# All x tiles asked for first, six at a time, with the adjacency of block 0 and the masks of unit 0 moved behind them

## The reference

```
h   = x @ W                      per head: 2048 x 64
s1  = h @ a1,  s2 = h @ a2       one score per node and head
e   = leaky_relu(s1[i] + s2[j], slope 0.2)
att = softmax over j of (e where adj[i, j] > 0, else -9e15)
out = layernorm(x + concat over heads of (att @ h))
```

## Time and profile before

| | |
|---|---|
| median of 3 runs | 3051.29 us |
| profiled execution | 3049.79 us |
| its span | 3048.1 us |
| busy: PE, VectorE, ScalarE, GpSimd | 2650.5, 2729.3, 2417.2, 841.0 us |
| L473, the products of h | 462.1 us |
| L574, ScalarE's compares | 2179.6 us |
| L807 + L814, the masks on VectorE | 616.5 + 583.9 us |

### The profile page before, as it was taken

How to read it: one execution, slowest core, us unless ns; L and a number is a source line. 1 busy time by engine, 2 the same in 40 slices (tenths; PEclk the granted TensorE clock), 3 DMA queues, 4 the chain that set the end, 5 groups by cost and what they waited for, 6 DMA issues and landing times.

```text
span 3048.1 us, 94883 instructions
## 1 busy us (share of the span) xinstructions
PE 2650.5 (87%) x36162; PEld 2275.6 (75%) x36162; DVE 2729.3 (90%) x4505; ACT 2417.2 (79%) x4038; POOL 841.0 (28%) x1011
## 2 busy tenths in 40 slices
PE   4898889989898898988989889898888988889885
PEld 2498875888668885788848888488874988758885
DVE  4899988999889998899988999889998999889996
ACT  2399973999649995599937998389973999739994
POOL 3522116121252213322143221512215121162211
PEclk9999999999999999999999999999999999999998
DMA  6346633575435654267542665337644476345763
GB/s 167 87 104 163 160 103 97 127 168 141 116 83 131 163 137 136 56 155 165 131 111 68 161 163 127 97 84 166 160 112 112 100 160 159 103 105 120 165 144 89
DMA packets 281095, 388.25 MB, mean 127 GB/s; under 512 B 161856, under 2 KB 161856, under 8 KB 280672
## 3 DMA queue, kind: packets, MB, share of 16 engines
q1 hardware_dynamic: 253536, 315.24, 39.3%
q0 software_dynamic: 27136, 67.12, 12.8%
HBM read 313.52 MB, written 34.14 MB: 114 GB/s over the span
## 4 chain that ended last, share of the span: by engine, by line
DVE 40%; issue 25%; PE 23%; ACT 6%; DVEq 2%; POOL 0%; DMA 0%; ACTq 0%; POOLq 0%
DVE m_pos L807 8%; PE ps L473 8%; PE ps L499 7%; DVE both L644 7%; PE ps L529 6%; ACT m_pos L574 6%; DVE m_pos L793 5%; DVE both L634 3%; DVE total L650 3%; DVE m_neg L814 2%; DVE xmax L625 2%; DVE y L674 2%; DVE prod L776 1%; DVE prod_d L779 1%; PE ps L410 1%
## 5 line engine op out<-in xcount | busy, mean ns | idle before, releaser
L574 ACT ACTIVATE m_pos<-ps,s_steep 128x512 fp8e4<-128x512 f32 x3584 | 2179.6, 1081 | 419.9 <-PE ps L424 309.6
L499 PE MATMUL ps<-b_both,m_pos 128*128 128x130 f16 x16384 | 1030.2, 223 | 242.0 <-DVE both L634 220.4
L499 PEld LDWEIGHTS ps<-b_both,m_pos 128*128 128x128 fp8e5 x16384 | 978.6, 99 | 275.0 <-issue 273.8
L529 PE MATMUL ps<-d_both,m_neg 128*128 128x130 f16 x16384 | 989.8, 222 | 46.5 <-DVE both L644 46.1
L529 PEld LDWEIGHTS ps<-d_both,m_neg 128*128 128x128 fp8e5 x16384 | 966.5, 99 | 74.2 <-issue 64.1
L807 DVE TENSOR_TENSOR m_pos<-m_pos,maskT 128x1024 uint32<-128x1024 uint32 x512 | 616.5, 1242 | 78.0 <-ACT m_pos L574 44.0
L814 DVE TENSOR_TENSOR m_neg<-m_pos,maskT 128x2048 uint32<-128x2048 uint32 x256 | 583.9, 2281 | 0.4
L473 PE MATMUL ps<-W_sb,xT 128*128 128x512 f32 x1024 | 462.1, 613 | 39.6 <-DVE prod_d L779 39.6
L540 ACT ACTIVATE adj_cut<-adj_in 128x1024 fp8e4<-128x1024 int32 x264 | 363.7, 1429 | 130.1 <-DMA adj_in<-in_adj 130.1
L970 POOL TENSOR_TENSOR den_scaled<-den_inv,bound 128x4 f32<-128x4 f32 x256 | 62.2, 243 | 1456.7 <-DVE den_inv L652 1396.1
L473 PEld LDWEIGHTS ps<-W_sb,xT 128*128 128x128 f32 x1024 | 200.4, 197 | 295.7 <-issue 240.5
(11 more groups left out here) (89 smaller groups left out, 1396.1 us busy)
## 6 DMA issues: line engine op xcount, KB each, us to landing
adj_in<-in_adj SPq DMA_DIRECT2D x266, 512.0 KB, 5.0
s_bc<-s_rows SPq DMA_DIRECT2D x258, 256.0 KB, 3.8
x_in<-in_x SPq DMA_DIRECT2D x144, 256.0 KB, 5.2
x_sum<-in_x POOLq DMA_DIRECT2D x128, 256.0 KB, 5.9
y<-in_x POOLq DMA_DIRECT2D x32, 1024.0 KB, 9.8
out<-y SPq DMA_DIRECT2D x32, 1024.0 KB, 7.3
maskT<-adj_cut SPq DMA_TRANSPOSE x264, 4.2
W_sb<-in_L_gnn_W SPq DMA_DIRECT2D x4, 256.0 KB, 7.2
```

The source lines that it names most:

```text
L499: mm = pe.matmul(acc, mask, b_both[:, j, h, :, :], start=(j == 0), stop=(j == JC - 1))
L529: mm = pe.matmul(acc, mask, d_both[:, j, h, :, :], start=(j == 0), stop=(j == JC - 1))
L574: ins = nc.scalar.activation(chunk(m_pos[h % 2], j, 0, BLK), ps[:, BANK_S1 + h % 2, :], ACT.Relu, bias=s2_steep[:, j, h:h + 1], scale=STEE ...
```

## The change

The x tiles of batch 0 get six buffers: the two of x_in and, lent for the prologue, the 8 KB per partition of m_neg[0] (`first_x`). SP asks for x0 and x1, then W, a1 and a2, then x2 to x15, each as soon as the tile six before it has been used. The adjacency pieces 0 and 1 follow all x tiles; pieces 2 to 7 and all eight turns follow the stores and loads of s1. On ScalarE the eight cuts go behind the exponentials, and `copy_s1` goes ahead of them. On TensorE the sum of |W| goes behind the turn of tile 11. On VectorE the masks of unit 0 go from the prologue into the loop, behind split 4 and only for b = 0; and in every batch the compare of unit 1 moves from behind split 1 to behind split 5, its make_pos from behind splits 4 and 6 to behind 7 and 9, its make_neg from behind 9 to behind 10.

```
+    FIRST = 6
+        def first_x(i):
+            if i % FIRST < 2:
+                return x_in[i % FIRST][:]
+            return m_neg[0][:].rearrange("p c i -> p (c i)").bitcast(F32)[:, (i % FIRST - 2) * F:(i % FIRST - 1) * F]
...
             for i in range(JC):
-                if i == 2:
+                if i >= FIRST:
+                    sp.wait_ge(x_turned, at(x_turned, i - FIRST + 1))
+                    sp.wait_ge(x_maxed, at(x_maxed, i - FIRST + 1))
+                    sp.wait_ge(x_added, at(x_added, i - FIRST + 1))
+                sp.dma_start(first_x(i), x_tiles[i // 2, i % 2]).then_inc(first_loaded[i % FIRST], 16)
+                if i == 1:
                     ...
-                if i < 2:
-                    load_piece(i, i % 2, i // 4, i // 2 % 2)
-                load_x(i, i % 2, i // 2)
-                if 2 <= i < 2 + PIECES:
-                    q = i - 2
-                    turn_piece(q, q % 2, 0, q // 2)
-                    load_piece(i, i % 2, i // 4, i // 2 % 2)
+            for i in range(2):
+                load_piece(i, i % 2, i // 4, i // 2 % 2)
             store_s1(0)
             sp.wait_ge(s1_stored, 16 * KB)
             load_s1(0, 0)
             load_s1(1, 1)
+            for q in range(PIECES):
+                turn_piece(q, q % 2, 0, q // 2)
+                i = q + 2
+                load_piece(i, i % 2, i // 4, i // 2 % 2)
...
             for i in range(JC):
-                turn_x(i, i % 2, i // 2)
-            pe.wait_ge(w_abs_made, 1)
...
+                turn_x(i, first_x(i), first_loaded[i % FIRST], i // FIRST, i % 2)
+                if i == JC - 5:
+                    pe.wait_ge(w_abs_made, 1)
...
             for i in range(JC):
-                if i < PIECES:
-                    cut_piece(i, i % 2, i // 2)
                 copy_xT(i, i % 2, i * P)
             copy_scores(0)
+            copy_s1(0)
             exponentials(0)
-            copy_s1(0)
+            for i in range(PIECES):
+                cut_piece(i, i % 2, i // 2)
             act.wait_ge(s2_turned, 1)
             compare(0, 0)
...
-            make_masks(0, 0, maskT[0], 0, 0)
...
                     split_chunk(b, jc)
-                    if jc == 1:
+                    if jc == 4:
+                        with dve.If(b < 1):
+                            make_masks(0, 0, maskT[0], 0, 0)
+                    if jc == 5:
                         compare(b * UNITS + 1, 1, b * (UNITS // 2))
-                    if jc in (4, 6):
-                        make_pos(b * UNITS + 1, 1, maskT[0], jc // 2 - 2)
-                    if jc == 9:
+                    if jc in (7, 9):
+                        make_pos(b * UNITS + 1, 1, maskT[0], jc // 2 - 3)
+                    if jc == 10:
                         make_neg(b * UNITS + 1, 1, maskT[0])
```

More of the change, by code:

```diff
@@ L186, in gat_kernel @@
         x_loaded = [sem(f"x_loaded{i}") for i in range(2)]
+        first_loaded = [sem(f"first_loaded{i}") for i in range(FIRST)]
         s1_stored = sem("s1_stored")
@@ L304, in load_x @@
             def load_x(xi, slot, pair):
-                if type(xi) is int:
-                    sp.wait_ge(x_added, at(x_added, xi - 1))
                 sp.wait_ge(x_turned, at(x_turned, xi - 1))
@@ L380, in _ @@
                 sp.wait_ge(piece_turned[slot], at(piece_turned[slot], 16 * (NBLK + 1) * IT))
-                sp.wait_ge(x_loaded[slot], 16 * (NBLK * IT + JC) // 2)
+                sp.wait_ge(x_loaded[slot], 16 * NBLK * IT // 2)
                 sp.wait_ge(s1_loaded[slot], 16 * (B * UNITS // 2 + 1))
@@ L386, in _, with turn_x @@
         def _(pe):
-            def turn_x(xi, slot, nth):
+            def turn_x(xi, tile, loaded, nth, slot):
                 pe.wait_ge(xT_copied, at(xT_copied, xi - 1))
-                pe.wait_ge(x_loaded[slot], 16 * (nth + 1))
+                pe.wait_ge(loaded, 16 * (nth + 1))
                 for fc in range(FC):
                     mm = pe.transpose(ps[:, BANK_X + slot, fc * P:(fc + 1) * P],
-                                      x_in[slot][:, fc * P:(fc + 1) * P], ident[:])
+                                      tile[:, fc * P:(fc + 1) * P], ident[:])
                 mm.then_inc(x_turned, 1)
@@ L446, in _ @@
             for i in range(JC):
-                turn_x(i, i % 2, i // 2)
-            pe.wait_ge(w_abs_made, 1)
-            for fc in range(FC):
-                mm = pe.matmul(ps[:, 0, :], ones[:], y[0][:, fc, :], start=(fc == 0), stop=(fc == FC - 1))
-            mm.then_inc(w_abs_summed, 1)
+                turn_x(i, first_x(i), first_loaded[i % FIRST], i // FIRST, i % 2)
+                if i == JC - 5:
+                    pe.wait_ge(w_abs_made, 1)
+                    for fc in range(FC):
+                        mm = pe.matmul(ps[:, 0, :], ones[:], y[0][:, fc, :], start=(fc == 0), stop=(fc == FC - 1))
+                    mm.then_inc(w_abs_summed, 1)
             turn_x_sum(0)
@@ L483, in _ @@
                             pe.wait_ge(hi_d_made, b * JC + JC - 1)
-                            turn_x(JC * (b + 1), 0, (b + 1) * (JC // 2))
+                            turn_x(JC * (b + 1), x_in[0][:], x_loaded[0], b * (JC // 2), 0)
                             pe.wait_ge(tiny_made, b + 1)
@@ L512, in _ @@
                             t = TILE_UNIT.index(unit)
-                            turn_x(JC * (b + 1) + t, t % 2, (b + 1) * (JC // 2) + t // 2)
+                            turn_x(JC * (b + 1) + t, x_in[t % 2][:], x_loaded[t % 2], b * (JC // 2) + t // 2, t % 2)
                         if unit == XSUM_UNIT:
@@ L621, in _, with max_x @@
             V = nc.vector
-            def max_x(xi, slot, nth, col):
-                dve.wait_ge(x_loaded[slot], 16 * (nth + 1))
-                V.tensor_reduce(xmax[:, col:col + 1], x_in[slot][:], AX.X, ALU.max,
+            def max_x(tile, loaded, nth, col):
+                dve.wait_ge(loaded, 16 * (nth + 1))
+                V.tensor_reduce(xmax[:, col:col + 1], tile, AX.X, ALU.max,
                                 apply_absolute_value=True).then_inc(x_maxed, 1)
@@ L844, in _ @@
             for i in range(JC):
-                max_x(i, i % 2, i // 2, i)
+                max_x(first_x(i), first_loaded[i % FIRST], i // FIRST, i)
                 if i == 4:
@@ L910, in _ @@
                             t = TILE_UNIT.index(unit)
-                            max_x(JC * (b + 1) + t, t % 2, (b + 1) * (JC // 2) + t // 2, t)
+                            max_x(x_in[t % 2][:], x_loaded[t % 2], b * (JC // 2) + t // 2, t)
                         if unit == XSUM_UNIT + 1:
@@ L936, in _, with add_first_x @@
             G = nc.gpsimd
-            def add_first_x(i, slot, nth):
+            def add_first_x(i):
                 pool.wait_ge(x_added, at(x_added, i))
-                pool.wait_ge(x_loaded[slot], 16 * (nth + 1))
-                G.tensor_tensor(x_sum[:], x_sum[:], x_in[slot][:], ALU.add).then_inc(x_added, 1)
+                pool.wait_ge(first_loaded[i % FIRST], 16 * (i // FIRST + 1))
+                G.tensor_tensor(x_sum[:], x_sum[:], first_x(i), ALU.add).then_inc(x_added, 1)
             def add_x(xi, t, odd, pair):
@@ L997, in _ @@
             for i in range(JC):
-                add_first_x(i, i % 2, i // 2)
+                add_first_x(i)
             clear_x_sum(0)
```

## The result

The changed kernel takes 3059.45 us (median of 12 runs, 3055.31 to 3062.41) against 3051.67 us (12 runs of the kernel before beside them). The ratio is 1.0024, with a 95% interval of 1.0015 to 1.0033: 7.8 us slower. The profiled execution took 3057.72 us with a span of 3055.7, 7.6 more than the span before.

A forecast was written before the change was run, and what follows sets the result against it. TensorE was taken to bound batch 0's products, VectorE batches 1 to 7 from split 9 on. +0.8 us in batch 0 and +7.9 in the later batches gave +8.7, so 3059 us, range 3051 to 3065.

The forecast's parts named there:

- The sum: Whole kernel: +0.8 us in batch 0 and +7.9 us in batches 1 to 7, together +8.7 us.
- Start of the scores: Prologue: the chain of scores starts at 42 us, bounds 39 to 45, where it started at 63.19 before.
- x2's maximum: Prologue, VectorE: comes at 12 to 16 us, with x2 asked for at about 10 and landing at 14.
- the eight steps of VectorE: Prologue: eight steps of maximum, product and sum, four at 2.59 us and four at 1.94, 18.1 us in all.
- The rule quoted in the prediction: Prologue: VectorE instructions with two SBUF inputs and GpSimd instructions reading SBUF exclude each other; four long steps, 2.6 us.
- The start from idle: TensorE at L410 (now L420): it starts from idle at 1.2 GHz, adding 1.8 us to the scores.
- Cuts and compare: ScalarE, batch 0: eight cuts of 25.1 us and compare 0 of 8.3 us hold product 2 until 91.4 us.
- The end of batch 0: Split 15 starts at 142.8 us against 141.97, +0.8 us; the whole gain of the prologue is eaten.
- ScalarE's last cut of the next block: Batch 0: ends some 43 us after product 2's start and 8 us before split 15, so hidden.
- Batches 1 to 7: VectorE behind split 9: a make_pos that wasn't there costs 1.13 us a batch, +7.9 us in all.
- TensorE's wait ahead of the second sum group: Batch 1, ahead of the second L499 group: a wait of about 3.4 us in place of 2.27.
- The branch: VectorE behind split 4, skipped in batches 1 to 7: falls into a wait of about 1 us, taken as costing nothing.

The follow-up runs named there:

- the last version: Changed kernel with compare 0 ahead of the cuts, batch 0's masks behind splits 9 and 11 to 13, later batches at old places; 3026.27 us, ratio 0.9921.

## Why the prediction was right, and where it wasn't

The time (3059 against 3059.45), the direction and the main cause held: the gain of the prologue is held back at product 2, and the later batches pay behind split 9.

That the time came out within half a microsecond is luck. The sum was +0.8 and +7.9. The spans show -1.1 and +7.9, and beside them -1.9 between split 0 and split 9 and +2.7 in the phases of the units, which the sum did not have; the three misses nearly cancel.

- **Start of the scores.** Predicted 42 us, measured 40.31; TensorE's wait of 28.45 us and its releaser, compare 0, are as predicted. x2's maximum came at 14.75, against a landing put at 14; that is two errors that cancel, since x2 was asked for at 7.21 and not at 10, and took 7.5 us to land, not 4. The term that was off is the eight steps of VectorE: I let GpSimd's additions lengthen four of them to 2.59 us, 18.1 in all. They took 17.0. L870 kept its 0.68 in six of the eight steps (1.15 and 1.78 in the other two), and GpSimd's additions took up to 7.35/4 = 1.84 us in place of the 1.48 I had reckoned with. So the one that was held up was mostly GpSimd, and it was busy until 38.5, not 34.7. TensorE waited for it: L412 started at 38.52, took 1.86 us at 1.2 GHz (granted clock 0.50) in place of 0.95, and L420 followed at once at 40.31, 0.3 us after VectorE's last step. The rule quoted in the prediction fits the trace; whom it costs I had wrong.
- **The start from idle.** L420 took 5.60 us at a mean granted clock of 0.64, against 3.64 at 1.00: +1.96 where 1.8 was forecast.
- **Cuts and compare.** Predicted 33.4 us from the end of the exponentials, measured 32.6 (56.34 to 88.95). Rounds were put at 7.1 us; they took 7.1, 6.6 and 6.7. The run with compare 0 first shows that this wait, and not the adjacency, held product 2; product 2 started 25.5 us earlier and the time fell by 10.8, since the adjacency is the next wait, as expected there.
- **The end of batch 0.** Split 15 was predicted at 142.8 and started at 140.87. The exponentials ended 1.7 us earlier than forecast, cuts and compare took 0.8 less, and product 2 to split 15 took 51.9 us in place of 51.4. Products 8 and 9 waited 1.11 and 0.35 us, where 0.95 and 0.6 were laid out. ScalarE's last cut of the next block ended 9.7 us before split 15, hidden as predicted.
- **Batches 1 to 7.** +7.9 predicted, +7.92 measured between split 9 and split 15. But I gave it to the make_pos alone. The runs show two moves that each cost this much or more: the make_neg behind 10 opens a wait of about 1 us at split 10 (+1.04 a batch by itself), and the make_pos behind 9 adds 1.13 us of work (+2.07 by itself, with the longer make_neg). Together they cost 1.13, since the one fills the other's gap. The weak step is that I laid VectorE's splits out against product 9 and took the next wait for gone, in place of asking what had covered it. The sum came out right because in the changed kernel the make_pos does fill it.
- **TensorE's wait ahead of the second sum group** stayed at 2.27 us, where I had said 3.4; this sign was wrong. Counted from split 9, the low parts of product 14 and of 15 both came 1.13 later, so the distance between them is the same, and the delay shows up earlier: a wait of 0.59 ahead of L401, and 0.97 in place of 0.64 ahead of L510.
- **The branch** cost nothing that can be seen between split 9 and split 15, in this kernel or in the one with six more.

What no run separates is the part of the six buffers and the part of the new order in SP's list in the earlier start of the scores.

## What to carry to other kernels

When work is moved along an engine that waits for another at regular places, lay out both engines and find the last wait: work ahead of it is free as far as the waits there reach, work behind it is paid in full, and work taken from between two such places leaves a wait behind. A change for the first pass of a loop should not change the order that all passes run; here 1.1 us won in batch 0 stood against 1.13 us lost in each of seven batches. And before a prefetch is judged, ask which wait stands next in line, here a product that waited for a bank whose reader had been queued behind the work that was moved.

## What the runs showed of the hardware

TensorE's restart isn't the same every time, and its length follows the granted clock. After the 28.45 us of idle the clock was 0.54 for the first 3.45 us (nearly all at 1.2 GHz), then 1.00 (2.4 GHz), in the views by stretch that answer to the earlier trace rows:

```profile
88.95:92.40 3.45, 3.45 (x5) 1.58 (x6) 0.00 (x0) 3.45 (x6) 0.00 (x0) 0.54 0.00 0
92.40:112.00 19.60, 18.97 (x45) 8.09 (x43) 15.72 (x21) 6.47 (x12) 7.61 (x7) 1.00 0.27 65
```

Products 2 to 7 took 22.42 us there and 23.93 in the run with the make_pos behind split 8, for the same 48 matmuls; in that run the clock was 0.50 from 91.02 to 97.20.

In unit 0 of the later batches TensorE restarts after its 2.27 us wait. From there to `spread_s1` it took 4.49 us in six of the seven batches before and 2.87 in the seventh; after the change 4.14 to 5.42, in sum 32.5 against 29.8. That is +2.7, the whole of the fourth line of the table. In the run with compare and make_pos moved it was 5.2 to 5.4 in all seven. The granted clock tells these lengths apart. Here are batch 1 before, batch 1 of the last version, and batch 1 of the run with compare and make_pos moved; the third figure from the end is the clock:

```profile
511.10:515.59 4.49, 4.49 (x53) 4.49 (x53) 0.00 (x0) 0.00 (x0) 1.94 (x2) 0.62 0.67 156
489.55:492.42 2.87, 2.87 (x53) 2.87 (x54) 0.00 (x0) 0.00 (x0) 1.95 (x2) 1.00 0.46 167
513.65:518.85 5.20, 5.20 (x53) 5.20 (x53) 0.00 (x0) 0.00 (x0) 1.94 (x2) 0.53 0.57 143
```

The second line of the table goes the same way. Before the change, split 0 to split 9 took 28.77 us at a mean clock of 0.94 in batch 1 and 29.2 to 30.1 at 0.88 or 0.89 in the other six; after it, four batches took 28.55 to 28.78 at 0.90 to 0.94 and three 29.4 to 29.6 at 0.88.

Three of the kernels vary over 8 to 11 us between their runs: compare 0 ahead of the cuts, the make_pos behind split 8, and only the make_neg moved. In the last of them the two fastest runs (3052.90 and 3056.58 us) had a mean granted clock of 0.975 and 0.974, and the three slowest (3061.95 to 3063.19) 0.967 to 0.969. So in that kernel the time goes with the clock. What decides when the clock falls and rises, and whether a step of 1 us shifts it, none of these runs tells.
